# Row sums of the third softmax: added up on GpSimd, reduced by TensorE once per head group

## What is computed

```python
kernel3 = jax.nn.softmax(jnp.einsum('bhmd,bhnd->bhmn', Q_l, K), axis=-1)
SV = jnp.matmul(jnp.matmul(kernel1, iterative_inv(kernel2)), jnp.matmul(kernel3, V))
```

## Time and profile before

| | |
|---|---|
| runs | 2398.06, 2398.17, 2401.6 us; median 2398.17 |
| profiled execution | 2398.65 us |
| its span | 2396.9 us |
| TensorE busy | 2142.2 us (89%), 26607 matmul records |
| VectorE busy | 1480.8 us (62%) |
| ScalarE busy | 995.4 us (42%) |
| GpSimd busy | 661.0 us (28%), 902 instructions |
| granted TensorE clock, mean | 0.972 of 2.4 GHz |

### The profile page before, as it was taken

One profiled execution on the slowest core, in us unless ns is written; L12 is line 12 of the kernel. 1 busy time (PEld: TensorE's weight loads), 2 busy tenths in 40 slices (PEclk: granted clock), 3 DMA queues, 4 the chain that ended last, 5 costly groups with the idle time before them and its releaser, 6 DMA issues.

```text
span 2396.9 us, 62050 instructions
## 1 busy us (share of the span) xinstructions
PE 2142.2 (89%) x26607; PEld 1403.2 (59%) x26607; DVE 1480.8 (62%) x3341; ACT 995.4 (42%) x1746; POOL 661.0 (28%) x902
## 2 busy tenths in 40 slices
PE   1589999999999999999999999999999999999955
PEld 1354756657475665747566574756657475565724
DVE  4466666575666667566666756666675666666531
ACT  1335344453534445354444535444453544445220
POOL 2112142231414223141322314132231413222041
PEclk9889999999999999999999999999999999999978
DMA  3312021120302103030210303021030302102010
GB/s 75 77 29 72 11 80 37 33 76 11 107 11 79 38 29 80 11 107 11 79 39 26 83 11 107 11 78 40 27 82 11 107 11 77 41 24 68 11 36 18
DMA packets 99866, 117.35 MB, mean 49 GB/s; under 512 B 19916, under 2 KB 70613, under 8 KB 99575
## 3 DMA queue, kind: packets, MB, share of 16 engines
q1 hardware_dynamic: 99592, 113.39, 17.8%
HBM read 36.99 MB, written 16.78 MB: 22 GB/s over the span
## 4 chain that ended last, share of the span: by engine, by line
PE 67%; DVE 13%; SPq 6%; ACT 6%; issue 3%; POOL 2%; DMA 1%; DVEq 1%; POOLq 0%; ACTq 0%
PE NS L865 10%; PE ringF L1081 10%; PE ringA L763 8%; PE ringF L1066 7%; SPq L373 6%; PE KV L946 5%; PE ringA L1032 5%; PE ringF L1114 3%; PE ringA L908 2%; DVE stage L1505 2%; PE ringA L932 2%; PE ringF L763 2%; PE ringF L1116 2%; ACT E L620 2%; PE ringF L1062 2%
## 5 line engine op out<-in xcount | busy, mean ns | idle before, releaser
L1081 PE MATMUL ringF<-x,H 128*128 128x257 f16 x1536 | 261.0, 273 | 0.0
L1429 DVE TENSOR_REDUCE mx<-ringA 128x8 f32<-128x512 f32 x256 | 175.6, 686 | 114.4 <-PE ringA L908 114.1
L1081 PE MATMUL ringF<-H 128*128 128x128 f16 x1536 | 233.7, 220 | 1.4 <-DVE H L1516 1.4
L612 ACT ACTIVATE E<-ringA,score_scale 128x512 f32<-128x512 f32 x256 | 175.3, 685 | 117.9 <-PE ringA L932 117.9
L763 PE MATMUL ringA<-xT,wqkv 128*128 128x512 f16 x768 | 177.9, 382 | 18.2 <-DMA KS<-KS 11.8
L620 ACT ACTIVATE E<-ringA,score_scale 128x512 f32<-128x512 f32 x256 | 158.6, 684 | 76.0 <-PE ringA L963 76.0
L1066 PE MATMUL ringF<-wd,x2T 128*128 128x512 f16 x768 | 190.0, 384 | 0.0
L1482 DVE SCALAR_TENSOR_TENSOR X<-X,NS 128x320 f32<-128x320 f32 x160 | 78.1, 488 | 180.7 <-PE NS L865 175.5
L1415 DVE TENSOR_REDUCE mx<-ringA 128x1 f32<-128x512 f32 x256 | 162.7, 684 | 31.3 <-PE ringA L899 31.0
L427 POOL TENSOR_SCALAR vtmp<-mv,eps_ffn 128x8 f32<-128x8 f32 x16 | 5.1, 316 | 628.1 <-DVE mv L1261 628.1
L427 POOL TENSOR_SCALAR vtmp<-mv,eps_ln 128x8 f32<-128x8 f32 x32 | 9.9, 310 | 608.6 <-DVE mv L1261 594.6
(11 more groups left out here) (251 smaller groups left out, 4634.2 us busy)
## 6 DMA issues: line engine op xcount, KB each, us to landing
KS<-stage SPq DMA_DIRECT2D x384, 64.0 KB, 2.0
QS<-stage SPq DMA_DIRECT2D x384, 64.0 KB, 2.0
xin<-in_L_attn_x_dram SPq DMA_DIRECT2D x16, 1024.0 KB, 6.8
xres<-in_L_attn_x_dram SPq DMA_DIRECT2D x16, 1024.0 KB, 7.9
out_dram<-yout SPq DMA_DIRECT2D x16, 1024.0 KB, 5.4
QS<-LB SPq DMA_DIRECT2D x16, 512.0 KB, 4.4
E<-in_L_attn_w_qkv_dram SPq DMA_DIRECT2D x1, 768.0 KB
E<-in_L_ffn_Wd_dram SPq DMA_DIRECT2D x2, 256.0 KB
```

What stands on the lines that cost most here:

```text
L612: A(E[:, k % ESLOTS, :], ps[:, :], ACT.Exp, scale=score_scale[:, 0:1]).then_inc(freed["s3"].sem, 1)
L1081: ins = MM(dst, H[:, a, t, own], src, start=first and i == 0, stop=last and i >= 4, skip_group_check=True)
L1429: V_.reduce_max(mx1[:, t, 8 * h:8 * h + 8], take(b, "m1", k)[:, :].rearrange("p (a m) -> p a m", a=8), AX.X)\
```

## The change

The ones are no longer applied to each tile of exponentials. GpSimd adds the tiles up, element by element, in a new fp32 buffer `E3sum` (a view of the first half of `stage`, free at that time): per head group one copy and then additions, 15 tiles in all. Tile 15, the last one, is not added. Behind the loop `sum_exponentials3` on TensorE applies the ones to the two sums and to tile 15. ScalarE's `exp3(k)`, k >= 8, now also waits for GpSimd to have read the slot. On GpSimd the additions stand ahead of `norm1(b + 1)`, and on ScalarE `halves1` moves by one Newton step.

```diff
+        E3sum = stage[:, 0, :, :].rearrange("p b n -> p (b n)").bitcast(F32).rearrange("p (g n) -> p g n", g=2)
...
+            def sum_tiles3(b):
+                pool.wait_ge(stk[2].sem, stk[2].at(b, 12))
+                for k in range(2 * T - 1):
+                    g, t = k // T, k % T
+                    pool.wait_ge(freed["s3"].sem, freed["s3"].at(b, k + 1))
+                    if t == 0:
+                        ins = pool.tensor_copy(E3sum[:, g, :], E[:, k % ESLOTS, :])
+                    else:
+                        pool.wait_ge(e_sum.sem, e_sum.at(b, k))
+                        ins = pool.tensor_tensor(E3sum[:, g, :], E3sum[:, g, :], E[:, k % ESLOTS, :], ALU.add)
+                    ins.then_inc(e_sum.sem, 1)
...
                     norm2(b - 1)
+                sum_tiles3(b)
                 if more:
                     norm1(b + 1)
...
                     act.wait_ge(kv_full.sem, kv_full.at(b, k - ESLOTS + 1))
+                    act.wait_ge(e_sum.sem, e_sum.at(b, k - ESLOTS + 1))
...
                     act.wait_ge(kv_full.sem, kv_full.at(b, 2 * T))
+                    act.wait_ge(ks_full.sem, ks_full.at(b, 2))
...
-                    if more and k < 2:
-                        halves1(b + 1, (k,))
+                    if more and 1 <= k < 3:
+                        halves1(b + 1, (k - 1,))
...
-                for i in range(2):
+                for j in range(GP):
+                    p = g * GP + j
+                    ins = MM(KV[32 * j:32 * j + 32, 2 * g * P:(2 * g + 1) * P], V[:, t, p, :],
+                             E[:, k % ESLOTS, j * P:(j + 1) * P], start=t == 0, stop=t == T - 1, skip_group_check=True)
+                ins.then_inc(kv_full.sem, 1)
+
+            def sum_exponentials3(b, g):
+
+                pe.wait_ge(e_sum.sem, e_sum.at(b, (2 * T - 1) if g else T))
+                tiles = [E3sum[:, g, :]] + [E[:, (2 * T - 1) % ESLOTS, :]] * g
+                for n, tile in enumerate(tiles):
                     for j in range(GP):
-                        p = g * GP + j
-                        ins = MM(KV[32 * j:32 * j + 32, (2 * g + i) * P:(2 * g + i + 1) * P], onesf[:, :] if i else V[:, t, p, :],
-                                 E[:, k % ESLOTS, j * P:(j + 1) * P], start=t == 0 and i == 0, stop=t == T - 1,
-                                 skip_group_check=True)
-                ins.then_inc(kv_full.sem, 1)
+                        ins = MM(KV[32 * j:32 * j + 32, (2 * g + 1) * P:(2 * g + 2) * P], onesf[:, :], tile[:, j * P:(j + 1) * P],
+                                 start=False, stop=n == len(tiles) - 1, skip_group_check=True)
+                ins.then_inc(ks_full.sem, 1)
...
                 for k in range(14, 16):
                     sum_values(b, k)
+                for g in range(2):
+                    sum_exponentials3(b, g)
...
-                dve.wait_ge(kv_full.sem, kv_full.at(b, 2 * T))
+                dve.wait_ge(ks_full.sem, ks_full.at(b, 2))
```

More of the change, by code:

```diff
@@ L256, in sandwich_kernel @@
         kv_full = sig("kv_full", 2 * T)
+        e_sum = sig("e_sum", 2 * T - 1)
+        ks_full = sig("ks_full", 2)
         w_done = sig("w_done", 3)
```

## The result

| | before | changed |
|---|---|---|
| runs of this comparison | 11 | 11 |
| median, us | 2397.58 | 2411.73 |
| lowest to highest, us | 2394.52 to 2401.60 | 2403.77 to 2418.99 |
| ratio, 95% interval | | 1.0055, 1.0039 to 1.0072 |

The changed kernel is slower by 0.55%, 14 us. It is also less steady: its executions spread over 15 us, those of before over 7. The profiled execution (2403.77 us, span 2402.1) is the fastest of the eleven, so its trace shows the loss's kind but not all of its size.

The account below looks back on a forecast made before the run. The prediction took TensorE, busy 89%, as paced by VectorE in stretches of the loop. Per batch -0.8 + 0.85 us made about 0; with the first batch's +0.8 and -1.7, -1 us in total: 2397.5 us, range 2382 to 2414.

Parts of the forecast that it names:

- GpSimd rival: Loop's end: TensorE waits for tile 14's sum, at 1.53 us per tile 1.0 us more per batch, 2414 us; chance 0.22.
- clock rival: Loop's second half: emptier TensorE falls to 1.2 GHz once per batch, 0.63 us each, 2407 us; chance 0.06.
- Removed and added on TensorE: Sixteen ones groups leave each batch, three return behind the loop: net 2.86 us less per batch if TensorE never waited.
- what the loop passes on: In the loop TensorE often follows VectorE, so only six of sixteen removed groups count: -0.8 us per batch.
- the third stretch: Loop time in which VectorE ran without a gap, 1101.64 to 1104.97; three ones groups were counted in it as no gain.
- GpSimd's pace: GpSimd in the loop: addition 1.27 us, pace 1.37 us, copy 0.85 us; wait for the last sum near zero, no slack.
- GpSimd against VectorE: Instructions with two SBUF operands collide with GpSimd's additions, in the loop and after it: +0.85 us per batch.
- Moved steps: The later `norm1` and `halves1` cost nothing, since TensorE is filled by gram matrices there.
- The sum: -0.8 + 0.85, about 0 per batch; first batch +0.8 and perhaps -1.7; total -1 us of 2398.65.
- The clock holds it there.: Batches follow at 139.95 us, 139.32 without m3's half-speed stretch; a few tenths' change per batch can be given back there.
- Faster, nobody is disturbed: GpSimd's additions disturb nobody, so -0.8 us stays in all 16 batches: 13 us less, 2385 us; chance 0.30.

Follow-up runs that it names:

- no_sums: The changed kernel without GpSimd's additions and all waits for them, the ones applied to three tiles only (13 left out of the sums): 2398.03 us, before beside it 2398.76.
- ones_and_sums: The kernel before plus GpSimd's additions (sums unused), their waits and the moved steps, the ones still applied to every tile on TensorE: 2402.68 us, before beside it 2398.76.
- fill_loop: The changed kernel with the four m1 matmuls of loop step 10 issued six times instead of once: 2398.76 us, before beside it 2398.76.
- before_reorder: The kernel before with VectorE's aggregation and sum-of-squares steps moved from loop steps 8 and 9 to behind step 11: 2390.26 us, before beside it 2398.43.
- reorder: The changed kernel with VectorE's aggregation and sum-of-squares steps moved from loop steps 8 and 9 to behind step 11: 2395.21 us, before beside it 2399.31.

## Why the prediction was wrong

The range (2382 to 2414 us) held the median, the sign of the likeliest case did not: no change was forecast, with 0.42, and it got slower. That the range held is in part luck. Its upper end was the time of the GpSimd rival, which hardly happened; the clock rival, which did, had 2407 us. And neither of the two signs that were to make the forecast wrong, additions of 1.5 us or loops below 27 us, came: none was set for the clock.

- *Removed and added on TensorE; what the loop passes on.* Right in kind. Six of sixteen groups were to count, -0.8 us per batch; no_sums shows -0.71. The match is closer than the working: the third stretch, which ends at 1104.97, holds a fourth ones group (at 1104.83), so by that rule five groups count, which gives only -0.5, and 1.4 - 0.66 = 0.74 was rounded up. TensorE's wait was to grow from 0.84 to about 1.5 us; it grew to 1.23.
- *GpSimd's pace.* Right in the addition (1.27 us forecast, 1.268 median), the copy was put 0.24 us too high (0.85, measured 0.61). The step between two additions is 0.14 us, not 0.10, so the pace is 1.41 and not 1.37; the 0.06 us that served as its lower bound stands between two memsets of different tiles, which don't depend on each other. No slack at `sum_exponentials3`, as it said, and a wait of 0.2 us.
- *GpSimd against VectorE.* The mechanism was right, the size was too high: +0.85 us per batch in the sum, +0.35 measured. L1394 (now L1422) took 0.70 us as the median, no loss; L1521 lost 0.15 in place of 0.25; L1462 lost 0.08, the addition of tile 14 beside it 0.27, and TensorE got the last sum 0.20 us late, in place of 0.4; `fold1_rows` lost nothing but once (L1469, longest 0.54), in place of 0.2. Not in my list was the small copy (L1404, now L1432), which lost 0.15 off the path though it has only one input. Those that came second lost 0.08 to 0.27 us, a fifth of an addition at most, not half.
- *Moved steps.* 0.08 us per batch in the middle, against nothing. It appears in no_sums and in ones_and_sums too, so it's neither the additions nor the lighter TensorE. The move of `halves1` is common to them all and the likeliest cause; no run moved it alone.
- *The sum.* With these sizes the undisturbed batch is 0.28 us shorter, and at that the change would have been about 4 us faster.
- *The clock.* This is the step that failed: a term of the time that stood at nothing in the sum, and at a chance of 0.06 among the rivals. The chance rested on the ground that the trace of before showed full clock in the whole loop, at the same time as it forecast that TensorE's wait there would nearly double and a quarter of its matmuls would go. It took the absence of low stretches for a margin. And the price, 0.63 us from the m3 stage, was too low for the loop, where it is 1.0 us, or over 2 when it lasts longer. fill_loop gives its size: 13 us in the median, although its repeats cost some 2 us in the first batch.
- *"The clock holds it there."* Wrong. The batch isn't held at 139.95 us: before_reorder shortened the middle loops by 0.55 us and the whole kernel by 8 us, about what 14 such loops make. In before the regular 139.95 us was an undisturbed batch (139.32) plus one low stretch in the m3 stage, no more.
- *Rivals.* "Faster, nobody is disturbed" fell with the collisions and the clock. "GpSimd becomes the bound" happened in the changed kernel only as the 0.20 us of waiting for the last sum. "The clock" happened.

Partly open: why the changed kernel's executions spread from 2404 to 2419 us. Only the fastest has a trace, but each has its mean granted clock. Three others at 2404 to 2405 us have 0.970 or 0.971. Six at 2411.69 to 2418.99 us have 0.961 to 0.966, the slowest the least. The traced one has 0.958 and one at 2417.23 us 0.949; in the traced one a low stretch of 51 us ahead of the first loop makes up 0.011 of that. So the slower executions did have the lower clock for longer. That they lose it in the loop would fit (seven such loops cost about 11 us here), but where it was lost wasn't seen, nor why a given loop falls and its neighbour, with the same wait, doesn't. Not separated either: whether the longer wait alone would do it, since no run has the wait of 1.23 us with the ones in place.

## What to carry to other kernels

An engine that is 89% busy may still be paced by another in stretches: count what is removed only where the waiting engine isn't already following someone. When work is taken from TensorE around an existing wait, ask what the wait and the thinner work do to its clock; a few repeated matmuls inside the wait tell whether the clock is the cause, at no cost where the wait is long enough to hold them. And before giving work to an idle engine, move the small steps that make the wait: that was worth 8 us here and left nothing for GpSimd to win.

## What the runs showed of the hardware

- A wait of 1.23 us on TensorE, busy for 0.79 us of the 2 us around it, was followed by the lower clock (0.50) in 7 of 14 middle loops of the changed kernel and in 7 of 14 of no_sums. With a wait of 0.84 us and the ones in place (before, ones_and_sums) it never was, nor with two waits of 0.70 us and the ones gone (reorder). The length of one wait isn't all: in the m3 stage of before the clock fell behind waits of 0.72, 0.30 and 0.22 us.
- A low stretch costs 0.63 us in the m3 stage of before, 1.0 us in the changed kernel's loop, and 2.1 to 2.5 us there where it lasts twice as long.
- A GpSimd addition of 128x512 fp32 in place takes 1.268 us, a copy 0.61 us, and additions that each use the one before start 1.41 us apart.
- VectorE instructions with two SBUF operands beside GpSimd's additions lose 0.08 to 0.33 us as the median in the changed kernel and ones_and_sums, 0.45 (G) and 0.7 us (the first sum-of-squares step) in reorder, 1.08 us at worst (L1551 in reorder, 1.25 in place of 0.17); as the Trainium skill's page "SBUF — State Buffer", section "Who interferes with whom", has it, the maxima with their input in PSUM lost nothing (0.686 us in the mean before, 0.684 after).
